# Casting transfers for the FFN weights, and the gate tail inside its own tile

## The reference

```python
# attention: 16 heads of 64, window of the 64 tokens before t, sigmoid instead of softmax
q, k, v = x @ wq, x @ wk, x @ wv;  q, k = rope(q), rope(k)
tau = sigmoid(scores / 8) * mask;  msg = sum(tau * v) / clip(sum(tau), 1e-6)
out = rms_norm(x + msg @ wo, norm_scale)
# FFN: 8 experts of 1408, the best 2 per token by router, and a shared one of 2816
router = xf @ Wg;  top_logits, idx = top_k(router, 2);  probs = softmax(top_logits)
h = silu(xf @ W1[e]) * (xf @ W2[e]);  y = sum_e w[:, e] * (h @ W3[e])
y = y + (silu(xf @ Ws1) * (xf @ Ws2)) @ Ws3
```

## Time and profile before

| | us |
|---|---|
| median of 2 executions | 7675.62 (7420.46 and 7930.78) |
| the profiled execution | 7224.98 |
| its span on the slowest core (6) | 7223.4 |
| spans of the 8 cores | 7206.3 to 7223.4 |
| TensorE busy | 5742.8 (80%) |
| VectorE, ScalarE, GpSimd busy | 2019.0, 1370.5, 1030.2 |

### The profile page before, as it was taken

How to read it: one execution, slowest core, us unless ns; L and a number is a source line. 1 busy time by engine, 2 the same in 40 slices (tenths; PEclk the granted TensorE clock), 3 DMA queues, 4 the chain that set the end, 5 groups by cost and what they waited for, 6 DMA issues and landing times.

```text
span 7223.4 us, 77319 instructions; the slowest of 8 cores (7206.3 to 7223.4 us)
## 1 busy us (share of the span) xinstructions
PE 5742.8 (80%) x27147; PEld 2634.1 (36%) x27626; DVE 2019.0 (28%) x3830; ACT 1370.5 (19%) x2437; POOL 1030.2 (14%) x904
## 2 busy tenths in 40 slices
PE   2565465456546778877889999998999999999999
PEld 0332223232222333333334444443444444444444
DVE  2344334434431222222222222222222222222222
ACT  3322322223232222222210111101010111011110
POOL 0000000000001111111221222212121212122221
PEclk9677577666758889988999999999999999999999
DMA  3000000000025564455532111123112122211111
GB/s 120 31 2 31 30 25 8 30 31 2 18 70 197 179 201 146 166 184 182 197 117 86 65 81 65 81 85 119 68 77 97 58 88 105 87 65 81 65 81 56
DMA packets 99098, 627.41 MB, mean 87 GB/s; under 512 B 11538, under 2 KB 22100, under 8 KB 83364
## 3 DMA queue, kind: packets, MB, share of 16 engines
q1 hardware_dynamic: 64804, 538.28, 20.5%
q0 software_dynamic: 10624, 42.08, 1.7%
q10 hardware_dynamic: 23296, 42.08, 1.6%
HBM read 493.82 MB, written 128.58 MB: 86 GB/s over the span
## 4 chain that ended last, share of the span: by engine, by line
PE 68%; DMA 12%; DVE 8%; ACT 8%; issue 3%; DVEq 1%; ACTq 1%; SPq 0%; POOLq 0%
PE B L1092 20%; PE B L1101 20%; PE B L1150 16%; DMA stg<-w 7%; PE B L503 2%; PE B L794 2%; DMA stg<-ws 2%; PE B L569 2%; ACT msg_n L746 2%; PE B L879 1%; DMA out_fm<-y_q 1%; DMA x1s<-ln 1%; PE B L625 1%; PE B L613 1%; ACT w2b L983 1%
## 5 line engine op out<-in xcount | busy, mean ns | idle before, releaser
L1092 PE MATMUL B<-ln_q,w1b 128*128 128x512 bf16 x6900 | 1686.0, 385 | 411.7 <-DVE b_w L1120 156.1
L1101 PE MATMUL B<-ln_q,w2b 128*128 128x512 bf16 x6896 | 1660.7, 381 | 8.1 <-issue 0.7
L1132 POOL TENSOR_TENSOR h_w<-silu_g,b_w 128x512 bf16<-128x512 bf16 x880 | 1013.3, 1153 | 3786.6 <-DVE b_w L1120 2991.4
L1150 PE MATMUL B<-h_w,w3b 128*128 128x512 bf16 x6900 | 1518.6, 379 | 7.4
L1112 ACT ACTIVATE silu_g<-B 128x512 bf16<-128x512 f32 x880 | 525.2, 597 | 4001.1 <-PE B L1101 3537.7
L1092 PEld LDWEIGHTS B<-ln_q,w1b 128*128 128x128 bf16 x7040 | 692.9, 99 | 1261.0 <-issue 458.0
L1120 DVE TENSOR_TENSOR b_w<-B,bcast_sb 128x512 bf16<-128x512 f32 x704 | 486.1, 691 | 1973.4 <-PE B L1101 1873.1
L1101 PEld LDWEIGHTS B<-ln_q,w2b 128*128 128x128 bf16 x7040 | 693.2, 98 | 845.2 <-issue 26.1
L1150 PEld LDWEIGHTS B<-h_w,w3b 128*128 128x128 bf16 x7040 | 688.6, 98 | 830.8
L1158 DVE TENSOR_TENSOR y_q<-B,y_q 128x512 f32<-128x512 f32 x640 | 442.6, 692 | 1072.0 <-PE B L1150 1045.1
L417 PE MATMUL B<-arena_bf,onesc 128*1 128x512 bf16 x128 | 65.1, 509 | 313.3 <-ACT arena_bf L870 180.1
(11 more groups left out here) (149 smaller groups left out, 3088.9 us busy)
## 6 DMA issues: line engine op xcount, KB each, us to landing
stg<-w SPq DMA_DIRECT2D x128, 704.0 KB, 5.1
w1b<-w1c SPq DMA_DIRECT2D x30, 2816.0 KB, 16.5
w2b<-w2c SPq DMA_DIRECT2D x30, 2816.0 KB, 9.4
w3b<-w3c SPq DMA_DIRECT2D x30, 2816.0 KB
stg<-w SPq DMA_DIRECT2D x88, 512.0 KB, 4.4
w1c<-w1b SPq DMA_DIRECT2D x10, 2816.0 KB, 14.3
w2c<-w2b SPq DMA_DIRECT2D x10, 2816.0 KB, 21.7
w3c<-w3b SPq DMA_DIRECT2D x10, 2816.0 KB
```

What stands on the lines that cost most here:

```text
L1092: e.matmul(gbank[:], w1b[:, w1par * NCC * HE + cc * HE + hc * 128: w1par * NCC * HE + cc * HE + hc * 128 + 128], ln2_q[:, lq + cc * QT + t ...
L1101: e.matmul(bbank[:], w2b[:, cc * HE + hc * 128: cc * HE + hc * 128 + 128], ln2_q[:, lq + cc * QT + tb * TB: lq + cc * QT + tb * TB + TB], ...
L1132: e.tensor_tensor(h_w[:, tb * NHC * 512 + hc * 512: tb * NHC * 512 + (hc + 1) * 512], silu_g[:, sl * 512:(sl + 1) * 512], b_w[:, sl * 512: ...
L1150: e.matmul(yb[:], w3b[:, hc * 1024 + fc * 128: hc * 1024 + fc * 128 + 128], h_w[:, tb * NHC * 512 + hc * 512: tb * NHC * 512 + (hc + 1) * ...
```

## The change

- In the first quarter each weight matrix is loaded by one transfer from GpSimd's queue that reads fp32 from HBM and writes bf16 to SBUF. `stg`, `load_chunks` and the casts of L978 and L983 are gone. The three stores of the copies stay on SP, each behind its load.
- `emit_tail` is gone; its instructions stand at the end of their own tile, behind the stores of ln2. The router matmuls move behind the broadcasts and L894, L900, and write bank 6. The store of the gates is issued by ScalarE before the next tile's casts, and the lanes that the next tile waits for include it.
- All statistics use banks 4 and 5. `rows32` has no buffer of its own but lies in `arena32`, with a third row.
- L811 and L867 wait for all additions of their tile, where each waited for its own chunk; L845 signals once.

```diff
-        rows32_t = sbA("rows32", [1, 1024], F32)
-        rows32 = rows32_t[0:1, :]
+        rows32 = arena32[0:1, 2048:3584]
...
-            pe_st = ln_stats(4, 2)
-            if tail_pending is not None:
-                emit_tail(tail_pending)
-                tail_pending = None
-            ve_rows = ln_rowops(pe_st, 4, 2, rw=rows_bf_guard)
+            pe_st = ln_stats()
+            ve_rows = ln_rowops(pe_st)
...
-                     waits=[(ve, min(ve_pre_base + cc + 1, ve_pre))],
+                     waits=[(ve, ve_pre)] if cc == 0 else (),
...
-                     waits=[(ve, min(ve_x1_base + cc + 1, ve_x1))])
+                     waits=[(ve, ve_x1)] if cc == 0 else ())
...
-            pe_st2 = ln_stats(6, 7)
+            pe_st2 = ln_stats()
             pe_st2_prev = pe_st2
-            for tb2 in range(4):
-                for cc in range(NCC):
-                    b.op("tensor", lambda e, cc=cc, tb2=tb2:
-                         e.matmul(B[5][:, tb2 * 8:(tb2 + 1) * 8],
...
             l2_ts = b.dma_multi("scalar",
...
                                 waits=[(ve, ve_ln2)])
+
+            for tb2 in range(4):
+                for cc in range(NCC):
+                    b.op("tensor", lambda e, cc=cc, tb2=tb2:
+                         e.matmul(B[6][:, tb2 * 8:(tb2 + 1) * 8],
...
+            b.op("scalar", lambda e: e.activation(p2_sb[:], gd_sb[:], AF.Sigmoid), waits=[(ve, ve_gd)],
+                 inc=se)
...
+            w_ts = b.dma_multi("scalar", [(w_dram[:, t0:t0 + TILE], w_fmt[:])], waits=[(ve, ve.n)])
             snap = b.lane_snap("scalar")
+            w_fmt_free = snap
             ln1bf_free = snap
             ln132_free = snap
...
-        stg = sbC("stg", [128, 2 * HE], F32)
...
             if qn == 0:
                 g1, g2, g3 = w_srcs(en)
-                w1_ready[(qn, en)] = load_chunks(g1, NCC, HE, w1b, npar * NCC * HE, "scalar", w1free, se)
-                w2_ready[(qn, en)] = load_chunks(g2, NCC, HE, w2b, 0, "scalar", w2free, se)
-                w3_ready[(qn, en)] = load_chunks(g3, NHC, 1024, w3b, 0, "vector", w3free, ve)
+                w1_ready[(qn, en)] = b.dma(
+                    "gpsimd", w1b[:, npar * NCC * HE:(npar + 1) * NCC * HE]
+                    .rearrange("p (c h) -> p c h", c=NCC), g1, waits=w1free)
+                w2_ready[(qn, en)] = b.dma(
+                    "gpsimd", w2b[:].rearrange("p (c h) -> p c h", c=NCC), g2, waits=w2free)
+                w3_ready[(qn, en)] = b.dma(
+                    "gpsimd", w3b[:].rearrange("p (c h) -> p c h", c=NHC), g3, waits=w3free)
```

More of the change, by code:

```diff
@@ L910, in build_program @@
                                 waits=[(ve, ve_ln2)])
+            for tb2 in range(4):
+                for cc in range(NCC):
+                    b.op("tensor", lambda e, cc=cc, tb2=tb2:
+                         e.matmul(B[6][:, tb2 * 8:(tb2 + 1) * 8],
+                                  ln1_32[:, cc * 512 + tb2 * 128: cc * 512 + tb2 * 128 + 128],
+                                  wg32[:, cc * 8:(cc + 1) * 8],
+                                  start=(cc == 0), stop=(cc == NCC - 1)),
+                         waits=[(ve, ve_x1), bank_free[6]] if (tb2 == 0 and cc == 0) else (),
+                         inc=pe if (tb2 == 3 and cc == NCC - 1) else None)
@@ new lines, in build_program @@
+            pe_rt = pe.n
+            for j in range(8):
+                b.op("tensor", lambda e, j=j:
+                     e.transpose(B[7][:, j:j + 1].bitcast(BF16)[:, 0:1],
+                                 rows_bf[0:1, j * 128:(j + 1) * 128], identB[0:1, 0:1]),
+                     waits=[(ve, ve_rows2), bank_free[7]] if j == 0 else (),
+                     inc=pe if j == 7 else None)
+            pe_ab = pe.n
+            b.op("vector", lambda e:
+                 e.tensor_copy(ab_tm[:], B[7][:, 0:8].bitcast(BF16)[:, 0:16:2]),
+                 waits=[(pe, pe_ab)], inc=ve)
@@ new lines, in build_program @@
+            bank_free[7] = (ve, ve.n)
+            b.drain("vector")
+            for tb2 in range(4):
+                b.op("vector", lambda e, tb2=tb2:
+                     e.tensor_scalar(r_sb[:, tb2 * 8:(tb2 + 1) * 8], B[6][:, tb2 * 8:(tb2 + 1) * 8],
+                                     ab_tm[:, tb2:tb2 + 1], None, ALU.mult),
+                     waits=[(pe, pe_rt)] if tb2 == 0 else ())
+            b.drain("vector")
+            for tb2 in range(4):
+                b.op("vector", lambda e, tb2=tb2:
+                     e.scalar_tensor_tensor(r_sb[:, tb2 * 8:(tb2 + 1) * 8], cs_rep[:],
+                                            ab_tm[:, 4 + tb2:5 + tb2],
+                                            r_sb[:, tb2 * 8:(tb2 + 1) * 8], ALU.mult, ALU.add),
+                     inc=ve if tb2 == 3 else None)
@@ new lines, in build_program @@
+            bank_free[6] = (ve, ve.n)
+            b.drain("vector")
+            for tb2 in range(4):
+                b.op("vector", lambda e, tb2=tb2:
+                     e.max(out=srt_sb[:, tb2 * 8:(tb2 + 1) * 8], in_=r_sb[:, tb2 * 8:(tb2 + 1) * 8]))
+            b.drain("vector")
+            for tb2 in range(4):
+                b.op("vector", lambda e, tb2=tb2:
+                     e.tensor_tensor(gd_sb[:, tb2:tb2 + 1], srt_sb[:, tb2 * 8 + 1:tb2 * 8 + 2],
+                                     srt_sb[:, tb2 * 8:tb2 * 8 + 1], ALU.subtract),
+                     inc=ve if tb2 == 3 else None)
@@ new lines, in build_program @@
+            b.drain("vector")
+            for tb2 in range(4):
+                b.op("vector", lambda e, tb2=tb2:
+                     e.tensor_copy(wstack[:, tb2 * 16:tb2 * 16 + 8], w32[:, tb2 * 8:(tb2 + 1) * 8]))
+            b.drain("vector")
+            for tb2 in range(4):
+                b.op("vector", lambda e, tb2=tb2:
+                     e.tensor_tensor(wstack[:, tb2 * 16 + 8:tb2 * 16 + 16], w32[:, tb2 * 8:(tb2 + 1) * 8],
+                                     wstack[:, tb2 * 16:tb2 * 16 + 8], ALU.subtract),
+                     inc=ve if tb2 == 3 else None)
@@ new lines, in build_program @@
+            ve_ws = ve.n
+            for tb2 in range(4):
+                b.op("tensor", lambda e, tb2=tb2:
+                     e.transpose(B[7][0:16, tb2 * 32:tb2 * 32 + 64].bitcast(BF16)[0:16, 0:128]
+                                 if False else B[7][0:16, tb2 * 64:tb2 * 64 + 64].bitcast(BF16),
+                                 wstack[:, tb2 * 16:(tb2 + 1) * 16], identB[:]),
+                     waits=[(ve, ve_ws), bank_free[7]] if tb2 == 0 else (),
+                     inc=pe if tb2 == 3 else None)
@@ new lines, in build_program @@
+            pe_wt = pe.n
+            for tb2 in range(4):
+                b.op("vector", lambda e, tb2=tb2:
+                     e.tensor_copy(w_fmt[:, tb2 * 128:(tb2 + 1) * 128],
+                                   B[7][0:16, tb2 * 64:tb2 * 64 + 64].bitcast(BF16)),
+                     waits=([(pe, pe_wt)] + w_fmt_free) if tb2 == 0 else (),
+                     inc=ve if tb2 == 3 else None)
+            bank_free[7] = (ve, ve.n)
+            w_ts = b.dma_multi("scalar", [(w_dram[:, t0:t0 + TILE], w_fmt[:])], waits=[(ve, ve.n)])
@@ L1030, in build_program @@
+                w2_ready[(qn, en)] = b.dma("sync", w2b[:], w2c[en],
+                                           waits=w2free + (cache_st[en][1:2] if qn == 1 else []))
+                w3_ready[(qn, en)] = b.dma("sync", w3b[:], w3c[en],
+                                           waits=w3free + (cache_st[en][2:3] if qn == 1 else []))
         if n_q > 0:
```

168 lines of the change are left out of this document (72 added, 96 removed).

## The result

The changed kernel takes 7053.5 us at the median of 11 executions (lowest 7016.9); the kernel before takes 7978.4 at the median of 10 (lowest 7229.8). So compared, the ratio is **0.9646, interval 0.9581 to 0.9712**: the change makes the kernel 3.5% faster. The two profiled executions are 7224.98 and 7027.18 us, a ratio of 0.973. The nine such executions of before that the later runs hold took 7222 to 7239 us, the six of after 7017 to 7054; by their medians the gain is 2.8%. The three lowest times of before in the comparison itself are 7229.8, 7310.8 and 7324.7, so its 3.5% is rather high.

The account below looks back on a forecast made before the run. Weight preparation through SP's two-slot ring sets the first quarter's period. Change = 121.1/r - 617.7 us (nine periods, FFN start, first half -21); r = 0.2975 gives -211 from 7225: 7014 us, own range 6950 to 7080, whole range 6930 to 7800.

Parts of the forecast that it names:

- first half: Attention half, 8 tiles: reordered steps sum to -24 us, taken as -21 for unseen semaphore steps.
- (a): Squares of L811 wait for all eight additions instead of one each: +3.6 us a tile, 29 in all.
- (c): Gate tail moves from between the statistics and L430 to after the normalisation: -2.5 us, seven times, -17.
- The periods: Nine expert transitions of the first quarter, 149.1 us each before: each changes by 11.53/r - 59.1.
- the start of the FFN: First stg issue to first L1150, 169.2 us before: changes by 17.3/r - 64.8.
- The open rate r: MB/us of source bytes of a casting transfer on GpSimd's queue; taken as 0.2975 from y_q's load, break-even at 0.196.
- The two stops: TensorE stops twice per expert period: for w2's last cast, then 18.5 us because VectorE is held by w3's casts.
- list of signs: If right: w1b and w2b land within 20 and 45 us, periods near 126 us with one stop of about 11.
- (b): The 64 router matmuls move behind the broadcasts, beside L894 and L900: -4.5 us a tile, -36.
- The cast that slows the transfer: Rival at L1092's wait for w1 and w2: r 0.159 to 0.256, 7225 +- 144 us; chance 0.24.
- the one that becomes the bound: Rival at L1092's wait for w2b: slower by over 2%, 7576 us at r = 0.125; chance 0.34.
- hidden anyway: Rival for the weight transfers: stall vanishes at r over 0.42; lies in the first band's low end, no own chance.

Follow-up runs that it names:

- The late store: The changed kernel with the store of w1's bf16 copy also waiting for w2's load: 6963.6 us.
- The probe: The changed kernel with four 2.88 MB loads on GpSimd's queue ahead of the FFN, plain and casting in turn: plain 10.7 us, casting 10.6.
- the part experiments: The kernel before with casting transfers for w3 alone, 7091.9 us, or for w1 and w2 alone, 7115.9 us.

## Why the prediction was right and where it was wrong

Two steps failed. One is the *level*, the time before the change from which the forecast was counted: the sum's -211 us went from the profiled 7225 and not from the median shown, 7676, so that the printed 7014 reads -8.6% against it, where -3.5% was measured. The other is a term of the sum, the *first half*: -21 us forecast, -0.9 measured, since steps (a) and (c) were priced at the durations of the upper clock level. The periods (-183 forecast, -179 measured) and the start of the FFN (-6.6 and -6.7) were right.

*The open rate r* was right for the slowest core. With r = 0.2975 the formula gives a landing of w2 at 11.53/0.2975 + 9.7 = 48.5 us; measured 48.2. The late store shows the two parts apart: 11.53/38.9 = 0.296 MB/us, and 9.3 us for the store. On the faster side the same loads land in 30.3 us, 0.38 MB/us. That the cores differ I had not foreseen; that y_q's load stood for the slower side, which sets the time, is in part luck. x_sb and ln_q, with 2 KB rows, were not of this kind. The probe shows why y_q's row could be used at all: the cast has no price there.

*The two stops* were right; the part experiments show each of them separately. Nine periods: formula 38.8 - 59.1 = -20.3 us each, -183 in all, measured -178.7 between the slowest cores; on the others the periods fell further, from 148 to between 119.7 and 125.2. My list of signs spoke of periods near 126 us; by the formula itself it should have been 128.8, and 129.2 was measured. The landings that it named, 20 and 45 us, should have been about 48 for w2 in the same way; measured 22.7 and 48.2. The start: 17.3/0.2975 - 64.8 = -6.6, measured -6.7.

*The first half* is the term that failed: -21 forecast, -0.9 measured (mean of all cores +2.3). The order of the steps was right, part by part, but each was priced at the duration that it has in one tile of before's trace. A matmul has two durations, and moving it changes which. Read between the same steps of all tiles, core 6 before and core 4 after:

| step | forecast | measured |
|---|---|---|
| (a) last addition to the end of the sums, 2.86 us, now 8.18; 8 times | +29 | +43 |
| (b) end of the row operations to ln2's end, 15.8 to 18.5 us, now 11.1 to 11.4; 8 times | -36 | -46 |
| (c) ln2's end to the next casts, 4.2 us, now 14.6; end of the statistics to the end of the row operations, 16.6, now 6.7; 7 times | -17 | +4 |

Step (a) had the wait right (+3.6 us a tile) and left out that the sums behind it run at the lower clock (+1.7). Step (b) gave more than forecast, since the router was priced by tile 6, where it takes 10.2 us; in four of the eight tiles it takes 11.3 to 12.9. Step (c) had "the router and the transposes are done 0.9 us later" than ln2. VectorE's copy of ab_tm:

```profile
1614.90 4.87 DVE L787 TENSOR_TENSOR ln_bf<-ln_bf,B 128x512 bf16<-128x512 bf16 x8
1623.73 0.17 DVE L817 CAST ab_tm<-B 128x8 f32<-128x8 bf16 x1 [3.96 <-PE B L811]
```

It starts 4.0 us after ln2's end, 3.1 more than forecast, because the router runs at the lower clock from its first matmul to its last. I had charged the slow clock to the FFN's first matmuls and forgot it here, where TensorE idles more.

*The rest of the kernel* was forecast at no change and gave 11.5 us, at the ends of the three quarters: 5.8, 4.3 and 1.9. Why, was not tried. That the sum of -211 comes near the measured -198 is partly luck: this gain makes up for half of what the first half missed.

*The level* was the largest flaw of the number as printed. 7014 was worked out against the profiled 7225 (-2.9%) and lies 13 us from the profiled 7027 and 3 us below the lowest time of all. Read against the median shown, 7676, it says -8.6%, and the measured ratio says -3.5% (-2.9 to -4.2). Both executions behind that median (7420 and 7931) were longer than the profiled one, as the prediction says itself; it gives 7450 for their level and still prints 7014, so the printed time and the printed median don't form a ratio. The mechanism's -2.9% sits at the edge of the interval; the profiled pair shows -2.7%, the medians of 7222 to 7239 and 7017 to 7054 us show -2.8%.

*The rivals.* The cast that slows the transfer, and the one that becomes the bound, are both excluded by the probe. What speaks in their favour, w2's landing being the stop in after, is true, but at 12 us and not at 30 or more. The case "hidden anyway" needs 0.42 MB/us by my text, and I wrote that nothing reaches it; half the cores nearly do, at 0.38 MB/us and some 8 us for the store (core 0: w2 lands after 38.1 us, cover 37.1).

## What to carry to other kernels

In an engine's program-order queue the price of an instruction is not its duration but how long it waits times what stands behind it: eleven 0.7 us casts on VectorE stopped TensorE for 18 us per expert, because a PSUM-freeing multiply stood behind them, and taking them away alone gained 13 us a period. Give a load that another buffer allows earlier to the queue before, not beside, the one that is late: w1 issued one stage ahead removed the whole stop without a byte less. And when a step on TensorE is moved, ask what TensorE does just before its new place; price it at both clock levels.

## What the runs showed of the hardware that I had not expected

- A casting transfer on GpSimd's queue (fp32 to bf16, rows of 5632 B) took the time of a plain one of the same source bytes: 10.6 and 10.7 us for 2.88 MB read.
- The cores are not equal when all of them load. Medians from issue to landing of w1 and w2: 17.4 and 38.1 us on core 0, 21.9 and 43.8 on core 1, 22.7 and 48.2 on core 4. Of every two neighbouring cores (0 and 1, 2 and 3, and so on) one is the faster, and it is the one that began the FFN first, counted from its own first instruction (core 0 at 2129.6 us, core 1 at 2137.4); w2's medians show this for all four pairs in each of the ten traces in which w1 and w2 are loaded this way. Why the first is served better was not tried. The kernel before shows no such split: its periods are 147.8 to 149.1 us. The Trainium skill, "HBM Reference", section Specifications, says that the two cores of a domain share its bandwidth. The cores' parts are uneven here; whether the neighbours are the two of a domain no run here shows.
- A 2.88 MB store beside a load delayed it by 5 to 9 us: w2b's landing fell from 48.2 to 38.9 us on the slowest core and from 38.1 to 30.3 on the fastest side when w1's store moved out of its way.
- After 5.4 us of idle time the next eight 512-column sums took 626 ns each at a granted clock of 0.50, where behind 1.8 us they took 378 at 1.00. Matmuls that nobody reads, put into a 5.6 us gap, brought the router back from 361 to 325 ns and paid for themselves (22 us in 8 tiles).
